# A four-layer AdaLN network in one Trainium2 kernel: a norm in four units, output projections one tick later, preparation spread over more ticks

## What is computed

```python
sa, ca, ga, sb, cb, gb = modulation(L_c, L_wmod)
h = _layernorm(x) * (1 + ca) + sa
x = x + ga * attention(h)
h = _layernorm(x) * (1 + cb) + sb
x = x + gb * ffn(h)
```

## Time and profile before

| | |
|---|---|
| median of three runs | 3154.87 us (3151.2 to 3159.9) |
| the profiled execution | 3156.93 us, its span 3155.0 us |
| PE busy | 2817.9 us, 89% (25404 matmuls); weight loads 1886.5 us, 60% |
| DVE busy | 2159.4 us, 68% |
| ACT busy | 1694.9 us, 54% |
| POOL busy | 1047.2 us, 33% |

### The profile page before, as it was taken

The page is one execution under the profiler, slowest core; times in us unless marked ns, Lnnn a source line. Parts: engine busy times, 40 slices in busy tenths (PEclk is TensorE's granted clock), DMA queues, the critical chain, the costliest instruction groups (busy, mean ns, idle before and its releaser), DMA issues.

```text
span 3155.0 us, 68904 instructions
## 1 busy us (share of the span) xinstructions
PE 2817.9 (89%) x25404; PEld 1886.5 (60%) x25404; DVE 2159.4 (68%) x5846; ACT 1694.9 (54%) x4067; POOL 1047.2 (33%) x1444
## 2 busy tenths in 40 slices
PE   5999999989999999999997998989699978895885
PEld 2666666666666666666664554766466645553663
DVE  5888888856666566666665887444577768864557
ACT  2877777863333477777764666333145533223553
POOL 5888888720000011111213553121333310014323
PEclk8999999999999999999997999999899989996997
DMA  3011111122000011111114442000344432325640
GB/s 100 16 29 28 31 29 29 38 69 82 14 1 1 19 29 29 31 36 32 29 32 145 138 128 68 1 14 1 100 115 122 126 71 55 68 55 150 177 121 27
DMA packets 189836, 188.13 MB, mean 60 GB/s; under 512 B 14288, under 2 KB 166032, under 8 KB 188736
## 3 DMA queue, kind: packets, MB, share of 16 engines
q1 hardware_dynamic: 189504, 183.73, 22.3%
HBM read 130.36 MB, written 53.31 MB: 58 GB/s over the span
## 4 chain that ended last, share of the span: by engine, by line
PE 55%; DVE 19%; POOL 13%; issue 7%; ACT 2%; DMA 2%; SPq 1%; DVEq 0%; POOLq 0%; ACTq 0%
PE pb L174 50%; POOL big L974 3%; POOL big L948 3%; DVE big L2069 2%; PE pb L620 2%; DVE big L240 1%; POOL big L939 1%; DVE big L785 1%; POOL big L940 1%; SPq L1750 1%; ACT big L895 1%; DVE big L190 1%; POOL big L960 1%; POOL big L200 1%; DVE big L2539 1%
## 5 line engine op out<-in xcount | busy, mean ns | idle before, releaser
L174 PE MATMUL pb<-big 128*128 128x128 f32 (+13 forms) x20220 | 2538.2, 333 | 186.6 <-DVE big L2069 54.1
L174 PEld LDWEIGHTS pb<-big 128*128 128x128 f32 (+5 forms) x20220 | 1576.6, 146 | 938.0 <-issue 536.1
L171 ACT ACTIVATE big<-pb 128x512 f32<-128x512 f32 (+7 forms) x1444 | 828.3, 619 | 607.7 <-PE pb L174 343.7
L171 ACT ACTIVATE big<-pb,big 128x512 f32<-128x512 f32 (+2 forms) x504 | 308.6, 632 | 685.8 <-PE pb L174 545.7
L2069 DVE TENSOR_REDUCE big<-pb 128x4 f32<-128x1024 f32 (+1 forms) x256 | 278.2, 1087 | 121.5 <-PE pb L174 118.2
L185 POOL TENSOR_TENSOR big<-big 128x128 f32<-128x128 f32 x224 | 100.6, 465 | 689.3 <-DVE big L182 685.4
L895 ACT ACTIVATE big<-big 128x256 f32<-128x256 f32 x512 | 254.1, 498 | 74.2 <-DVE big L790 72.4
L895 ACT ACTIVATE big<-pb,big 128x128 f32<-128x128 f32 (+1 forms) x512 | 255.6, 513 | 64.0 <-DVE big L770 63.7
L974 POOL TENSOR_TENSOR big<-big 128x512 f32<-128x512 f32 x128 | 159.7, 1275 | 273.6 <-DMA big<-recip 273.6
L785 DVE CUSTOM_DVE_ANT_0 big<-pb,big 128x256 f32<-128x256 f32 x512 | 186.7, 421 | 90.6 <-PE pb L174 90.2
L1460 DVE SCALAR_TENSOR_TENSOR big<-pb,big 128x128 f32<-128x128 f32 x512 | 144.0, 344 | 145.8 <-PE pb L174 145.8
(11 more groups left out here) (136 smaller groups left out, 2290.0 us busy)
## 6 DMA issues: line engine op xcount, KB each, us to landing
big<-parts SPq DMA_DIRECT2D x96, 512.0 KB, 4.2
parts<-big SPq DMA_DIRECT2D x384, 96.0 KB, 2.3
big<-recip SPq DMA_DIRECT2D x64, 512.0 KB, 6.6
big<-comb SPq DMA_DIRECT2D x32, 512.0 KB, 8.3
parts<-big SPq DMA_DIRECT2D x192, 64.0 KB, 2.1
big<-gates SPq DMA_DIRECT2D x8, 1024.0 KB, 6.4
big<-in_wa SPq DMA_DIRECT2D x2, 2048.0 KB, 9.3
big<-in_wf SPq DMA_DIRECT2D x1, 3072.0 KB, 14.7
```

The source lines that it names most:

```text
L171: return e.activation(o, i, f, bias=bias, scale=scale)
L174: return e.matmul(o, l, r_, start=start, stop=stop, skip_group_check=True)
```

## The change

1. In both wide attentions `posts` puts c0 and c1 into ticks 6 and 7 of the block, not 5 and 6, and in the tail the same four steps are taken with these numbers. The tail's own ticks stay where they were.
2. The finish of a chunk of layer 1's experts becomes four units, at t % 8 = 1, 2, 3, 4 (`finish_at`): POOL's sum; DVE's statistics and POOL's 1/sqrt; DVE's normalization and POOL's product and sum; DVE's and POOL's residual. In each tick they stand behind the down product and ahead of the next chunk's pieces. Chunk 7's last three units become a guest (`own_end`) in ticks 1, 3 and 5 of narrow attention 2, behind the maxima of the tick before.
3. ScalarE's wait at the start of narrow attention 2 is taken out, and SP waits only for layer 1's last down product (`own_sync`) before it reads layer 3's condition and weights; the wait for all residuals and `second_gates` come behind the copy back of block 5.
4. Narrow attention 1's start is hosted in 15 steps, not 12: the two splits and the products of its first two blocks, which stood in steps 10 and 11, stand in steps 9, 10, 11 and 14 (ticks 121, 122, 123 and 126 of wide attention 1).
5. The preparation of the first two chunks of layer 2's experts is hosted in 29 steps, not 19, from tick 98 of narrow attention 2, not 116. Its gate pieces work in buffers of their own (`first_w1`, `first_w2`), and the three memsets of CTT and the wait for free memory (`mem_free`) move from `logits` to `spread`, and to SP.

The diff at its core (indentation is cut by twelve):

```diff
-    return [(step, t // 8 - 1) for step, late in (("recip", 0), ("turn", 1), ("scale0", 3), ("scale1", 4), ("c0", 5), ("c1", 6))
+    return [(step, t // 8 - 1) for step, late in (("recip", 0), ("turn", 1), ("scale0", 3), ("scale1", 4), ("c0", 6), ("c1", 7))
...
-tail = Guest(4, lambda i: take_tick(131 + i, 16, 17, 3 + i, ring=BK[6:8]),
-             lambda e, i: tensor_extra(e, 131 + i, 16, 17, 3 + i),
-             lambda e, i: vector_extra(e, 131 + i, 16, 17, 3 + i),
+left = (3, 4, 6, 7)
+tail = Guest(4, lambda i: take_tick(128 + left[i], 16, 17, left[i], ring=BK[6:8]),
+             lambda e, i: tensor_extra(e, 128 + left[i], 16, 17, left[i]),
+             lambda e, i: vector_extra(e, 128 + left[i], 16, 17, left[i]),
              lambda e, i: None,
-             lambda e, i: gpsimd_tick(e, 131 + i, 16, 17, 3 + i), tail_sync)
+             lambda e, i: gpsimd_tick(e, 128 + left[i], 16, 17, left[i]), tail_sync)
...
+    place(16384)
+    first_w1, first_w2 = alloc(512), alloc(512)
...
-    first = dict(zip(pieces + ["spread"], (0, 1, 2, 4, 6, 7, 8, 9, 10)))
-    second = dict(zip(pieces + ["spread"], (3, 7, 8, 10, 12, 14, 15, 16, 18)))
+    first = dict(zip(pieces + ["spread"], (0, 2, 4, 6, 8, 10, 12, 14, 22)))
+    second = dict(zip(pieces + ["spread"], (9, 11, 14, 16, 18, 20, 23, 25, 28)))
...
+def works(c):
+    return (first_w1, first_w2) if pairs and c < 2 else (w1, w2)
...
+    if u == nunit - 1 and X1 is None:
         e.wait_ge(y.free, y.n)
-        vector_finish(e, c)
-def vector_finish(e, c):
+        vector_residual(e, c)
+def vector_residual(e, c):
+    for i in range(4):
+        n = r0 + 4 * c + i
+        residual_vector(e, n, 4 * c + i, ACC[c % nr][:, i, :], 128).then_inc(gated, 1)
+def finish_at(t):
+    return (t - 9) // 8, (t - 9) % 8
...
+def vector_finish(e, c, step):
     s = c % nr
-    if X1 is not None:
+    if step == 1:
         e.wait_ge(x1_added, c + 1)
         stats_vector(e, own, [ACC[s][:, i, :] for i in range(4)], 4, x1_mean)
+    elif step == 2:
         e.wait_ge(x1_rstd, c + 1)
         for i in range(4):
             x = e.tensor_scalar(ACC[s][:, i, :], ACC[s][:, i, :], mv[:, 4 + i, 0:1], rs[:, 4 + i:5 + i],
                                 ALU.subtract, ALU.mult)
         x.then_inc(x1_normed, 1)
+    elif step == 3:
         e.wait_ge(x1_scaled, c + 1)
-    for i in range(4):
-        n = r0 + 4 * c + i
-        residual_vector(e, n, 4 * c + i, ACC[s][:, i, :], 128).then_inc(gated, 1)
+        vector_residual(e, c)
 def vector_hosted(e, i):
     if i == 0:
         weights_in(e)
         e.wait_ge(ld_tri, 16)
     for c, p in hosted_step(i):
-        if c == 0 and p == "logits":
+        if c == 0 and p == ("spread" if pairs else "logits"):
             start.mem_free(e)
-            if pairs:
-                for n in range(nr):
-                    e.memset(CTT[n][0:32, :], 1.0).then_inc(own.sem, own.up())
+        if pairs and c == 0 and p == "spread":
+            for n in range(nr):
+                e.memset(CTT[n][0:32, :], 1.0).then_inc(own.sem, own.up())
+            e.wait_ge(own.sem, own.n)
...
+        if k == 1 and t >= 9:
+            vector_finish(e, *finish_at(t))
...
+def gpsimd_residual(e, c):
+    for i in range(4):
+        e.wait_ge(gated, d0 + 4 * c + i + 1)
+        residual_gpsimd(e, r0 + 4 * c + i, 4 * c + i)
+def gpsimd_finish(e, c, step):
     s = c % nr
-    if X1 is not None:
+    if step == 0:
         y = slots["y", nunit * c + nunit - 1]
         e.wait_ge(y.free, y.n)
         for i in range(4):
             x = e.tensor_tensor(ACC[s][:, i, :], ACC[s][:, i, :], X1[:, 4 * c + i, :], ALU.add)
         x.then_inc(x1_added, 1)
+    elif step == 1:
         e.wait_ge(x1_mean, c + 1)
         rstd_gpsimd(e, own_g, 4, 4, x1_rstd)
+    elif step == 2:
         gb_ = lambda o: LNW[:, o:o + 128].unsqueeze(1).to_broadcast([128, 4, 128])
         e.wait_ge(x1_normed, c + 1)
         e.tensor_tensor(ACC[s], ACC[s], gb_(256), ALU.mult).then_inc(own_g.sem, own_g.up())
         e.wait_ge(own_g.sem, own_g.n)
         e.tensor_tensor(ACC[s], ACC[s], gb_(384), ALU.add).then_inc(x1_scaled, 1)
-    for i in range(4):
-        e.wait_ge(gated, d0 + 4 * c + i + 1)
-        residual_gpsimd(e, r0 + 4 * c + i, 4 * c + i)
+    elif step == 3:
+        gpsimd_residual(e, c)
...
+        start.mem_free(e)
...
-start = Guest((7, 9, 19)[k], lambda i: [take_piece(c, p) for c, p in hosted_step(i)],
+start = Guest((7, 9, 29)[k], lambda i: [take_piece(c, p) for c, p in hosted_step(i)],
               tensor_hosted, vector_hosted, scalar_hosted, gpsimd_hosted, sync_hosted)
-tail, guest = yield start, None
+def own_sync(e):
+    y = slots["y", T - 1]
+    e.wait_ge(y.full, y.n)
+own_end = Guest(3, nothing, lambda e, i: None, lambda e, i: vector_finish(e, 7, i + 1), lambda e, i: None,
+                lambda e, i: gpsimd_finish(e, 7, i + 1), own_sync) if k == 1 else None
+tail, guest = yield start, own_end
...
-guests_at = 126 if k == 1 else 116
+guests_at = 126 if k == 1 else 98
...
-                10: [(0, "qk0"), (0, "split"), (0, "v")], 11: [(1, "qk0"), (1, "split"), (1, "v")]}.get(i, [])
+                9: [(0, "qk0"), (0, "v")], 10: [(0, "split"), (1, "qk0")], 11: [(1, "v")], 14: [(1, "split")]}.get(i, [])
...
-    return {5: 0, 6: 1, 9: 2, 11: 3}.get(t, -1) if k == 1 else -1
+    return ({5: 0, 6: 1, 9: 2, 11: 3} if k == 1 else {1: 0, 3: 1, 5: 2}).get(t, -1)
...
-    if k == 2:
-        e.wait_ge(gated, 32 * k)
...
+        if tail_at(t) >= 0:
+            tail.scalar(e, tail_at(t))
...
-        e.wait_ge(gated, 32 * k)
-        second_gates(e, k)
+        tail.sync(e)
...
+        if k == 2 and b == 5:
+            e.wait_ge(gated, 32 * k)
+            second_gates(e, k)
...
-start = Guest(12 if k == 1 else 7, lambda i: [take_piece(b, piece, BK[6:8]) for b, piece in hosted_step(i)],
+start = Guest(15 if k == 1 else 7, lambda i: [take_piece(b, piece, BK[6:8]) for b, piece in hosted_step(i)],
```

More of the change, by code:

```diff
@@ L1320, in vector_gate @@
                 glv, gpv, gkv, cm = v3(gl), v3(gp), v3(gk), v3(CMB[c % nr])
+                w1, w2 = works(c)
                 if k == 0:
@@ L1463, in vector_down @@
                 x.then_inc(y.free, 1)
-                if u == nunit - 1:
+                if u == nunit - 1 and X1 is None:
                     e.wait_ge(y.free, y.n)
-                    vector_finish(e, c)
-            def vector_finish(e, c):
+                    vector_residual(e, c)
[6 more added lines that the diff above has]
+            def vector_finish(e, c, step):
                 s = c % nr
-                if X1 is not None:
+                if step == 1:
                     e.wait_ge(x1_added, c + 1)
                     stats_vector(e, own, [ACC[s][:, i, :] for i in range(4)], 4, x1_mean)
+                elif step == 2:
                     e.wait_ge(x1_rstd, c + 1)
@@ L1562, in scalar @@
                         guest.scalar(e, t - guests_at)
-            def gpsimd_finish(e, c):
+            def gpsimd_residual(e, c):
[3 more added lines that the diff above has]
+            def gpsimd_finish(e, c, step):
                 s = c % nr
-                if X1 is not None:
+                if step == 0:
                     y = slots["y", nunit * c + nunit - 1]
@@ L1589, in gpsimd @@
                 for t in range(T + 2):
-                    if t >= 2 and (t - 2) % nunit == nunit - 1:
-                        gpsimd_finish(e, (t - 2) // nunit)
+                    if k == 1 and t >= 9:
+                        gpsimd_finish(e, *finish_at(t))
+                    elif k != 1 and t >= 2 and (t - 2) % nunit == nunit - 1:
+                        gpsimd_residual(e, (t - 2) // nunit)
                     if t < T:
```

## The result

| | before | after |
|---|---|---|
| median | 3156.29 us (4 runs, 3151.2 to 3159.9) | 3134.49 us (4 runs, 3133.6 to 3137.5) |
| ratio, 95% interval | | 0.9934 (0.9917 to 0.9951) |
| profiled execution, its span | 3156.93, 3155.0 us | 3133.61, 3131.6 us |
| PE, DVE, ACT, POOL busy | 2817.9, 2159.4, 1694.9, 1047.2 us | 2804.7, 2163.2, 1690.9, 1045.6 us |

The account below looks back on a forecast made before the run. PE was taken to bound most stages, with DVE and POOL close behind in wide attention 0. Terms 6.4 - 6 - 2 - 10 - 7 - 2 = -20.6 gave 3136.3 us, 3134 from the median; range 3108 to 3150.

Parts of the forecast that it names:

- Wide attention 0: Moving c0 and c1 ends PE's waits for POOL but c1 waits for project's bank in tick 7: +6.4 us.
- Wide attention 1, blocks: In wide attention 1 DVE frees project's bank, so PE has no bank waits in the blocks: 0.
- Its end: End of wide attention 1: the 6.38 us wait for scale1 goes, some slow stretch too, about 2.4 set against: -6 us.
- Chunks 0 to 5: Layer 1's experts: per chunk, 3.0 us of PE waits are exchanged for a 2.7 us gate wait: -2 us.
- Contention of DVE and POOL: Layer 1's experts: by the skill's shared-interface rule each gate would take near 4 us, six chunks +3 instead of -2.
- Chunk 6: Layer 1's experts: PE's 9.12 us wait for layer 2's first norm goes but for 1 to 2 us: -10 us.
- Hand-over: Chunk 7 to narrow attention 2: first maximum comes at once, units in loops 2, 4, 6 cost +0.3, +1.1, +1.7: -7 us.
- End of narrow attention 2: Spreading layer 2's preparation from tick 98 loses 3.2 us in the ticks and wins 5 in the tail: -2 us.
- (a): Rival: every PE wait that goes is gained; 3101 us, or 3115 with wide attention 0 alone; chances 0.15 and 0.12.
- (b): Rival: layer 2's preparation in narrow attention 2 costs its upper bound, +14: 3148 us, no change to be told; chance 0.14.
- (c): Rival: PE is held at half speed from tick 98 of narrow attention 2: slower, 3164 us; chance 0.05.
- (d): Rival: the units of layer 1's experts do nothing, for chunks 6 and 7 too: 3151 us; chance 0.04.

Follow-up runs that it names:

- v5_w0: Changed kernel with the fourth v product of wide attention 0 in tick 5 instead of 7; 3113.3 us, ratio to before 0.9872.
- residual_late: Changed kernel with the residual unit of layer 1's experts at t % 8 = 6 instead of 4, behind the gate's tick; 3120.0 us.
- own_end_late: Changed kernel with the last three units of layer 1's experts in ticks 9, 11, 13 of narrow attention 2, not 1, 3, 5; 3136.8 us.
- split_old: Changed kernel with narrow attention 1's start in 12 steps as before, splits in ticks 122 and 123 of wide attention 1; 3136.0 us.
- prep_old: Changed kernel with layer 2's preparation as before, in 19 steps from tick 116 of narrow attention 2; 3140.0 us.
- c_back_w0: Changed kernel with c0 and c1 of wide attention 0 alone put back into ticks 5 and 6; 3128.1 us.

## Why the prediction was right

The sum was -20.6 and the span fell by 23.4, and no term had the wrong sign. But six of the ten stretches of the table are off by more than 2 us, in both directions: three came out 8.5 us worse than forecast in all, three 9.4 us better. Part of the close agreement is luck, all the more as the same code varies by 2 to 5 us between profiles in several stretches.

- **Wide attention 0 (+6.4, measured +6.6):** right in mechanism and size, for blocks without a norm (+1.08 to +1.1 against +0.9) and with one (-0.15 against -0.1). The forecast reached it by adding 1.0 for the bank and taking off 0.1: of the 0.9 us that PE waited for POOL, it let only 0.1 be gained, since DVE's L696 sets the end of tick 5. That is what came. It named the bank as the loss; v5_w0 shows that the idle time left in tick 5 is worth as much, 0.9 a block, once work is put there.
- **Wide attention 1, blocks (0, measured +3.8; 2 to 5 over nine profiles):** the step that failed. "PE has no such waits: 0 in the blocks" looked for a bank and found none. What grew by 2.1 us was the wait for exponentials, which this step had not looked at; another 1.7 us are PE's busy time, and their cause is open.
- **Its end (-6, measured -8.2; -5.3 to -8.3 over eight profiles):** right. Whether the 2.4 set against it for maxima and exponentials was too much, these profiles do not tell.
- **Chunks 0 to 5 (-2, measured -6.5):** the exchange of waits was exact: 17.8 us for 18.1 in all, 2.85 in the chunk shown against a forecast of 2.7. The other 6 us are not waits. In a chunk without a slow interval, the four intervals from the last down product on went from 18.5 to 18.0 us, 3.1 for six chunks, where the forecast had 0.3 each. The remaining 3.1 are slow intervals: in the kernel before four of those right behind the norm's wait took 2.24 to 3.37 us where the others had 1.75, 4.7 us together, at a granted clock of 0.97 for the stretch; after it one took 5.93 for 4.28, at 0.99. The wait for down products (2.4 us) was followed by half clock more often than the wait for the gate (2.8), though it is shorter. Why, no run here tells.
- **Contention of DVE and POOL.** The gate took 3.36 us beside POOL's last residuals (2058.21 to 2061.57) and 3.10 in residual_late without them; L1345 alone took 0.45 against 0.19, and the comparisons (L1065 and on) 0.42 to 0.43 in both. The Trainium skill (GPSIMD Engine Reference, Specifications) says that POOL contends with DVE instructions that have two SBUF inputs. The trace agrees in one such instruction, L1345, which overlapped POOL's last addition (L185, to 2059.04); POOL was done when the comparisons ran, and the gate of nearly 4 us worked out from that rule did not come. The norm's 3.28 against 1.11 us, which the prediction took for this rule, are TENSOR_SCALAR instructions with one tensor input, so they show that the two engines slow each other down, but not this case.
- **Chunk 6 (-10, measured -10.8)** right; the clock of this stretch went from 0.91 to 1.00.
- **Hand-over (-7, measured -4.4, and +2.1 up to tick 96):** the first maximum comes 8.3 us sooner, as said. The units cost 3.9 instead of 3.1; own_end_late shows 3.6 of it. The half clock lasts through the eight ticks (0.50 for 0.59), but they took no less at 0.58. The 2.1 later on is a stretch in which PE waited for a copy back (1.6 us) and then ran at half clock; in five of the ten profiles with this code, v5_w0 and split_old among them, it did not occur.
- **End of narrow attention 2 (-2, measured -5.8 by the two profiles):** the formula of a maximum plus its pieces held for the long ticks (4.6 to 5.6 us measured), 25.2 us over the base against 26.7 forecast. From the last maximum to the last value it took 15.1 us (to 2568.50) for 21.1, where the forecast had 16, and 1.6 more were won behind. What of this is the spread is open: prep_old shows a cost of 6 to 8 and a gain of 6 to 9, no net.
- **Rivals.** (a) is out: c_back_w0 shows the loss. When c0 was moved behind what PE had waited for, the waits of wide attention 0 did not end; they changed their cause. Yet v5_w0 and residual_late brought 21 and 14 us, so the rule of the Trainium skill (Perfetto Trace Analysis, Optimization Strategy), to look for PE's gaps and make what they wait for complete sooner, found the right places; it is the edits that must aim at the cause next in line. (b) and (c) did not occur: the spread lost nothing net, and the granted clock from tick 98 to the last maximum was 0.90. (d) is out too: the stretch of chunk 6 fell by 10.8 us.

## What to carry to other kernels

When work is moved out of a tick, ask two things: who ends the tick now (here DVE and ScalarE, so the tick got 2.2 us shorter where 1.9 of work and 0.9 of waiting had left it), and which shared ring the work joins in its new tick (here a fourth taker in a ring of three). The best place is a tick in which the full engine idles and the ring has a bank: one number in a tuple was worth 21 us by the medians, 24 by the blocks. In an in-order queue a unit with slack must not stand ahead of one that the bound engine waits for; two ticks later it cost nothing and gave 14 us. And a difference of 2 us between two profiles was often no more than the same code shows from profile to profile; the sum over many equal blocks told what the whole stage did not.
